# First group norm about an early average, constants on ScalarE's queue, half chunks, and first patches loaded behind their own block's store

## What is computed

```python
def _gn(v, G=32, eps=1e-5):           # group norm: 32 groups of 12 channels
    g = v.reshape(B_, G, C_ // G, H_, W_)
    m = jnp.mean(g, axis=(2, 3, 4), keepdims=True)
    s = jnp.var(g, axis=(2, 3, 4), keepdims=True)
    return ((g - m) / jnp.sqrt(s + eps)).reshape(v.shape)

# x: 1 x 384 x 192 x 192 float32
x = x + _L0_conv_ref(_gn(x), ...)   # 1x1 conv to q, k, v; 2x2 max pool; 3x3 depthwise; channel attention
                                    # with four top-k softmaxes; gelu; doubling; 1x1 projection
x = x + _L1_conv_ref(_gn(x), ...)   # depthwise 13x13 + 3x3 + identity, each with a batch norm
```

## Time and profile before

| | us |
|---|---|
| median of three runs | 2852.78 |
| the profiled execution | 2850.55 |
| its span, first to last instruction | 2848.7 |
| TensorE busy (90%) | 2575.4 |
| VectorE busy (89%) | 2523.7 |
| ScalarE busy (52%) | 1483.0 |
| GpSimd busy (3%) | 84.8 |

### The profile page before, as it was taken

The page is one execution under the profiler, slowest core; times in us unless marked ns, Lnnn a source line. Parts: engine busy times, 40 slices in busy tenths (PEclk is TensorE's granted clock), DMA queues, the critical chain, the costliest instruction groups (busy, mean ns, idle before and its releaser), DMA issues. The chain is left out here.

```text
span 2848.7 us, 50909 instructions
## 1 busy us (share of the span) xinstructions
PE 2575.4 (90%) x17291; PEld 1861.9 (65%) x17291; DVE 2523.7 (89%) x3511; ACT 1483.0 (52%) x1920; POOL 84.8 (3%) x155
## 2 busy tenths in 40 slices
PE   0039999999999999999999599998599999999998
PEld 0026666666666666666666366666499999999997
DVE  7968999999999999999999799999688888888884
ACT  0043354555554644555423277777566666666663
POOL 0020000000000000000000100000200000000000
PEclk9999999999999999999999799999799999999999
DMA  8965112332323223313000499997999999999996
GB/s 332 416 212 175 62 34 85 102 97 70 91 86 109 74 86 103 97 69 91 34 17 7 171 357 357 362 361 281 249 278 291 288 289 290 296 295 294 290 287 184
DMA packets 346041, 546.38 MB, mean 192 GB/s; under 512 B 133536, under 2 KB 244896, under 8 KB 345888
## 3 DMA queue, kind: packets, MB, share of 16 engines
q1 hardware_dynamic: 321984, 465.80, 52.0%
q10 hardware_dynamic: 23424, 77.08, 8.0%
q0 software_dynamic: 480, 1.51, 0.2%
HBM read 363.88 MB, written 180.44 MB: 191 GB/s over the span
## 5 line engine op out<-in xcount | busy, mean ns | idle before, releaser
L774 PE MATMUL qk_qb<-qk_xhi,whi 128*128 128x384 f16 x2592 | 846.2, 326 | 19.6 <-DVE qk_xlo L670 14.3
L774 PE MATMUL qk_qb<-qk_xlo,whi 128*128 128x384 f16 x2592 | 846.2, 326 | 0.0
L774 PE MATMUL qk_qb<-qk_xhi,wlo 128*128 128x384 f16 x2592 | 846.2, 326 | 0.0
L691 DVE SCALAR_TENSOR_TENSOR qk_dw<-qk_pool,qk_wd,qk_dw 128x768 f32<-128x768 f32 (+2 forms) x864 | 837.8, 1010 | 2.0 <-ACT qk_dw L543 2.0
L678 DVE TENSOR_REDUCE qk_pool<-qk_qb 128x192 f32<-128x768 f32 x432 | 412.2, 954 | 65.8 <-PE qk_qb L774 49.2
L1674 PE MATMUL cv_cb<-cv_hi,cv_toep 128*128 128x288 f16 x1536 | 346.8, 286 | 30.0 <-DVE cv_lo_last L1606 22.9
L774 PEld LDWEIGHTS qk_qb<-qk_xhi,whi 128*128 128x128 f16 x2592 | 254.0, 98 | 182.8 <-DVE qk_xlo L670 16.1
L774 PEld LDWEIGHTS qk_qb<-qk_xhi,wlo 128*128 128x128 f16 x2592 | 253.9, 98 | 168.2 <-issue 1.0
L774 PEld LDWEIGHTS qk_qb<-qk_xlo,whi 128*128 128x128 f16 x2592 | 254.0, 98 | 162.8 <-issue 1.0
L1680 PE MATMUL cv_cb<-cv_hi_next,cv_toep 128*128 128x288 f16 x1536 | 346.0, 287 | 0.0
L1549 ACT ACTIVATE cv_res<-cv_cb,cv_cst 128x288 f32<-128x288 f32 x384 | 187.5, 502 | 298.7 <-PE cv_cb L1680 237.1
(11 more groups left out here) (182 smaller groups left out, 3532.4 us busy)
## 6 DMA issues: line engine op xcount, KB each, us to landing
cv_toep<-toeplitz_scratch SPq DMA_DIRECT2D x384, 256.0 KB, 6.6
cv_raw<-patch_scratch SPq DMA_DIRECT2D x192, 325.0 KB, 7.5
st_x<-in_x SPq DMA_DIRECT2D x24, 2304.0 KB, 17.1
qk_xf<-in_x SPq DMA_DIRECT2D x72, 768.0 KB, 4.2
pr_xb<-in_x SPq DMA_DIRECT2D x24, 2304.0 KB, 10.1
out<-cv_rows ACTq DMA_DIRECT2D x72, 768.0 KB, 7.1
patch_scratch<-pr_turned SPq DMA_DIRECT2D x39, 832.0 KB, 9.3
patch_scratch<-cv_raw SPq DMA_DIRECT2D x36, 832.0 KB, 9.2
```

Source lines behind the costliest of these rows:

```text
L691: V.scalar_tensor_tensor(acc, pool[:, o, r + y:r + y + n, x:x + PW], wd[:, o, k:k + 1], acc, ALU.mult, ALU.add).then_inc(taps_done, 1)
L774: ins = nc.tensor.matmul(qbank[s % NQB][:, h, 0:2 * W], w[:, b, o * P:(o + 1) * P], x[:, par, j // 2, b, at_row:at_row + 2 * W], start=n = ...
```

## The change

1. In the statistics, the 24 transfers of weights and constants are issued by ScalarE's queue at its start; SyncE's queue holds chunks alone.
2. VectorE's `wlo` and tap preparation stand behind chunk 11 instead of chunk 3.
3. `group_affine` is gone. Ahead of the last round VectorE sums the records' means of chunks 0 to 19, TensorE averages the sums over the groups while the last four chunks run; the deviations of all records are taken about this early average `base`, and one pass of averages over two columns (`cols`) gives the correction `off` and the variance. It stands at the head of `stage_qkv`. Averages skip the pairs of blocks that share no group (seven matmuls instead of nine), in the second norm too.
4. The first two chunks are split in halves, with norms shared between ScalarE (6) and VectorE (6). Chunk 1 has a place of its own in `dw` (`second`), loaded at the stage's start; so chunk 2's load waits for chunk 0 only. GpSimd clears `dw` and what follows only when all halves are split; ScalarE waits for `padw` at unit 1.
5. TensorE runs 24 matmuls behind the averages in the q/k/v stage and 48 transposes at the start of the depthwise stage whose results nobody reads.
6. `conv.first_load` stands behind the store of block 0, ahead of those of blocks 1 and 2.

```diff
@@ stage_statistics, sync @@
-            sp.dma_start(wst[:, :, :], wT.rearrange("(b p) n -> p b n", p=P)).then_inc(w_in, 16)
-            sp.dma_start(kern[:, :, :, :], w_large.rearrange("(b p) o y x -> p b (o y) x", p=P)).then_inc(c_in, 16)
...
-            ahead.constants(sp)
@@ stage_statistics, scalar @@
+            act.dma_start(wst[:, :, :], wT.rearrange("(b p) n -> p b n", p=P)).then_inc(w_in, 16)
...
+            ahead.constants(act)
             act.wait_ge(w_in, 16)
@@ stage_statistics, vector @@
             statistics(0)
+            with dve.Fori(1, ROUNDS // 2) as r:
+                statistics(r)
             dve.wait_ge(whi_ready, 1)
...
-            with dve.Fori(1, STEPS // XBUFS) as r:
+            with dve.Fori(ROUNDS // 2, ROUNDS - 1) as r:
                 statistics(r)
+            records = stats[:, :, :, :].rearrange("p b n (two s) -> p b (n two) s", two=2)
+            dve.wait_ge(x_used, (ROUNDS - 1) * XBUFS)
+            V.tensor_reduce(sums[:, :], records[:, :, 0:KNOWN, 1], AX.X, ALU.add).then_inc(sums_ready, 1)
+            statistics(ROUNDS - 1)
+            dve.wait_ge(guess_done, 1)
+            chained(V.tensor_scalar(base[:, :], guess[:, 0:CB], 1.0 / KNOWN, None, ALU.mult))
+            dve.wait_ge(x_used, STEPS)
+            chained(V.tensor_tensor(dev[:, 0], records[:, :, :, 1],
+                                    base[:, :].unsqueeze(2).broadcast_to([P, CB, 2 * STEPS * REC]), ALU.subtract))
+            chained(V.tensor_tensor(dev[:, 1], dev[:, 0], dev[:, 0], ALU.mult))
+            V.tensor_reduce(part[:, 0], records[:, :, :, 2], AX.X, ALU.add)
+            V.tensor_reduce(cols[:, :, 0], dev[:, 0], AX.X, ALU.add)
+            chained(V.tensor_reduce(part[:, 1], dev[:, 1], AX.X, ALU.add))
+            V.scalar_tensor_tensor(cols[:, :, 1], part[:, 0], 2.0 / 512, part[:, 1], ALU.mult, ALU.add)
@@ stage_qkv @@
+        PIECES = [(h, k) for h in range(HALF) for k in range(2)]
+        BY_DVE = ((0, 1), (1, 1), (1, 2), (2, 1), (3, 1), (3, 2))
@@ stage_qkv, sync @@
             for b in range(CB):
-                load(1, b)
+                start.load_into(sp, second[:, b], 1, b, x2_in[b])
             for b in range(CB):
-                load(2, b)
+                sp.wait_ge(lo_half, b + 1)
+                sp.wait_ge(lo_ready, b + 1)
+                start.load(sp, 2, b)
@@ stage_qkv, scalar @@
+            nc.scalar.activation(root[:, :], var[:, :], ACT.Sqrt, bias=eps[:, :], scale=UNSCALE).then_inc(root_ready, 1)
...
-            for h in range(HALF):
+            for n in range(2 * HALF):
                 for b in range(CB):
-                    norm(h, b)
-                    high(h, 0, h, b)
+                    if (n, b) in BY_ACT:
+                        early_norm(n, b)
+                for b in range(CB):
+                    early_high(n, b)
@@ stage_qkv, gpsimd @@
+            gp.wait_ge(lo_half, HALF * CB)
+            gp.wait_ge(lo_ready, HALF * CB)
             G.memset(dw[:, :, 0:PW], 0.0).then_inc(zeroed, 1)
@@ stage_qkv, vector: off, var and mean from averages, sx from root, then @@
-            for h in range(HALF):
+            early_norm(0, 1)
+            early_norm(1, 1)
+            early_norm(1, 2)
+            for b in range(CB):
+                early_low(0, b)
+            early_norm(2, 1)
+            for b in range(CB):
+                early_low(1, b)
+            early_norm(3, 1)
+            early_norm(3, 2)
+            for n in range(2, 2 * HALF):
                 for b in range(CB):
-                    low(h, 0, h, b)
+                    early_low(n, b)
@@ stage_qkv, tensor @@
+            for o in range(CB):
+                near = [b for b in range(CB) if abs(b - o) <= 1]
+                for b in near:
+                    ins = nc.tensor.matmul(averages[:, 2 * o:2 * o + 2], member[:, b, o * P:(o + 1) * P], cols[:, b, :],
+                                           start=b == near[0], stop=b == near[-1])
+            ins.then_inc(avg_done, 1)
+            for n in range(WARM):
+                nc.tensor.matmul(qbank[1][:, 0, 0:2 * W], whi[:, 0, 0:P], whi[:, 0, 0:2 * W],
+                                 start=n == 0, stop=n == WARM - 1)
@@ stage_project, sync @@
-            sp.wait_ge(stored[0][0], 16 * (STEPS // 2 + 1))
-            sp.wait_ge(stored[1][0], 16 * (STEPS // 2))
-            conv.first_load(sp)
+                if b == 0:
+                    sp.wait_ge(stored[0][0], 16 * (STEPS // 2 + 1))
+                    sp.wait_ge(stored[1][0], 16 * (STEPS // 2))
+                    conv.first_load(sp)
@@ stage_depthwise, tensor @@
+            WARM = 48
+            for n in range(WARM):
+                nc.tensor.transpose(bbank[0][:, n % TPB * P:(n % TPB + 1) * P], ident[:, :], ident[:, :])
```

More of the change, by code:

```diff
@@ L162, in stage_statistics @@
-def stage_statistics(nc, x3, stats, wT, whi, wlo, w_large, w_small, norms, kern, scale, shift, ident, place, member, ahead):
+def stage_statistics(nc, x3, stats, base, cols, wT, whi, wlo, w_large, w_small, norms, kern, scale, shift, ident, place, member, ahead):
     XBUFS = 4
     REC = CHUNK // 512
+    ROUNDS = STEPS // XBUFS
+    KNOWN = (ROUNDS - 1) * XBUFS * REC * 2
     with ExitStack() as ctx:
@@ L320, in qkv_start, with stage_qkv @@
     start.xf, start.bq, start.bd, start.wd, start.c_in, start.x_in = xf, bq, bd, wd, c_in, x_in
-    start.constants, start.load, start.first_load = constants, load, first_load
+    start.constants, start.load, start.load_into, start.first_load = constants, load, load_into, first_load
     return start
-def stage_qkv(nc, start, whi, wlo, mean, rstd, ident, kern, inv_norm, v_dram, toep_dram, edge_dram, gram):
+def stage_qkv(nc, start, whi, wlo, base, cols, member, ident, kern, inv_norm, v_dram, toep_dram, edge_dram, gram):
     HALF = 2
@@ L351, in stage_qkv @@
     BANKS = 2 * QK
+    RECORDS = STEPS * (CHUNK // 512) * 2
+    HALVES = CHUNK // 2
     with ExitStack() as ctx:
@@ L377, in stage_qkv @@
         tbank = [ps(f"tb{i}", [P, 512]) for i in range(NTB)]
+        off, sq, var, root, mean = sb("off", [P, CB]), sb("sq", [P, CB]), sb("var", [P, CB]), sb("root", [P, CB]), sb("mean", [P, CB])
+        eps = sb("eps", [P, 1])
+        averages = tbank[0]
+        second = dw[:, :, :].rearrange("p r n -> p (r n)")[:, 0:CB * CHUNK].rearrange("p (b n) -> p b n", b=CB)
+        x2_in = [sem(f"x2_in{b}") for b in range(CB)]
+        link, eps_ready, avg_done, var_ready, root_ready = (sem("link"), sem("eps_ready"), sem("avg_done"), sem("var_ready"),
+                                                            sem("root_ready"))
+        act_norm, dve_norm, hi_half, lo_half = sem("act_norm"), sem("dve_norm"), sem("hi_half"), sem("lo_half")
         prep, zeroed = sem("prep"), sem("zeroed")
@@ L417, in wait_taps, with early, early_loaded, early_normed @@
             eng.wait_ge(taps_done, tap_index(u, o, k) + 1)
+        PIECES = [(h, k) for h in range(HALF) for k in range(2)]
+        BY_DVE = ((0, 1), (1, 1), (1, 2), (2, 1), (3, 1), (3, 2))
+        BY_ACT = tuple((n, b) for n in range(2 * HALF) for b in range(CB) if (n, b) not in BY_DVE)
+        def early(n, b):
+            h, k = PIECES[n]
+            return (xf[:, b] if h == 0 else second[:, b])[:, k * HALVES:(k + 1) * HALVES]
+        def early_loaded(eng, n, b):
+            h, k = PIECES[n]
+            eng.wait_ge(x_in[b] if h == 0 else x2_in[b], 16)
+        def early_normed(eng, n, b):
+            if (n, b) in BY_DVE:
+                eng.wait_ge(dve_norm, BY_DVE.index((n, b)) + 1)
+            else:
+                eng.wait_ge(act_norm, BY_ACT.index((n, b)) + 1)
         def run(eng, step):
@@ L728, in _ @@
             GRAM_AT = {3: (0, 3), 5: (3, NPX + 1)}
+            WARM = 24
+            for o in range(CB):
+                near = [b for b in range(CB) if abs(b - o) <= 1]
+                for b in near:
+                    ins = nc.tensor.matmul(averages[:, 2 * o:2 * o + 2], member[:, b, o * P:(o + 1) * P], cols[:, b, :],
+                                           start=b == near[0], stop=b == near[-1])
+            ins.then_inc(avg_done, 1)
+            for n in range(WARM):
+                nc.tensor.matmul(qbank[1][:, 0, 0:2 * W], whi[:, 0, 0:P], whi[:, 0, 0:2 * W],
+                                 start=n == 0, stop=n == WARM - 1)
             def transposes(u, par, o):
@@ L1283, in averages @@
                 for o in range(CB):
-                    for b in range(CB):
+                    near = [b for b in range(CB) if abs(b - o) <= 1]
+                    for b in near:
                         ins = nc.tensor.matmul(bank[:, o:o + 1], member[:, b, o * P:(o + 1) * P], values(b),
-                                               start=b == 0, stop=b == CB - 1)
+                                               start=b == near[0], stop=b == near[-1])
                 ins.then_inc(done, 1)
```

131 lines of the change are left out of this document (66 added, 65 removed).

## The result

The changed kernel takes **2856.66 us** (median of 20 runs, 2852.73 to 2859.47) where the kernel before takes 2852.60 in as many (2849.92 to 2854.93). The ratio is 1.0015 with an interval of 1.0009 to 1.0022: no gain, 4.1 us later, where 18 us less were forecast. The profiled execution (2858.81, span 2857.1) is 8.3 us behind that of before; each lies some 2 us to its own side of its median, so the pair of traces shows twice the difference of the medians.

What follows compares the result with a forecast made beforehand. TensorE was taken to bound the q/k/v and steady depthwise stretches, so gains had to come ahead of them: 11.3 us up to and through q/k/v plus 7.0 at the patch loads, 18.3 in sum, median 2834.5 us, range 2825 to 2843.

Steps and rivals of the forecast that it cites:

- the first part of its sum: Everything from the statistics through the q/k/v stage: 11.3 us gained, between 8 and 14.5.
- Rival (e): Statistics: small packets take turns with the chunks' big ones, making statistics 30 us longer instead of 4; 2860 us, chance 0.05.
- Statistics without that wait: Statistics with constants on ScalarE's queue and preparation moved: end at 159.1 us instead of 162.6, 3.5 gained (0 to 7.5).
- Early average: Group norm, from last statistics to first norm: 8.2 us against 18.6, 10.4 gained.
- Halves: First chunks of q/k/v: slot 2 starts 16.5 us behind the first norm instead of 21.3, 4.9 gained.
- Blank stores, chunk 3: Early q/k/v: later blank stores delay chunk 3, so the 4.9 us gain becomes a 6.3 us TensorE stall.
- the clock: TensorE behind the stall at chunk 3's copy: half-speed matmuls lose 2.4 us (0 to 3).
- Patch loads: Start of the depthwise stage, loads behind the first store: VectorE starts 8.7 us earlier, 7.0 net (3 to 11).
- the term for GpSimd: Depthwise start: GpSimd's memset, copies and sends fall on VectorE's first pieces and the tap loads; 1.7 us taken off.

Runs made afterwards that it cites:

- e1: Changed kernel with the nine last small transfers issued by ScalarE behind `whi` and `std` instead of ahead of them: 2842.94 us, ratio 0.9970.
- e4: Changed kernel with the 24 transfers of weights and constants back in SyncE's queue, VectorE's preparation left behind chunk 11: 2840.55 us, ratio 0.9963.
- e5: e1 with VectorE's preparation moved from behind chunk 11 to behind chunk 15: 2833.16 us, ratio 0.9939.
- e9: e7 with VectorE's reductions of the first two slots put ahead of the last half chunk's lows: 2825.66 us, ratio 0.9909.
- e8: e5 with GpSimd held in the depthwise stage until VectorE's third low part is made: 2833.38 us.
- e2: Changed kernel with every statistics chunk loaded by two transfers of 3 KB rows instead of one of 6 KB rows: 2837.82 us, ratio 0.9952.
- e3: Kernel before with only the eight first patch loads moved behind the store of block 0: 2846.04 us, ratio 0.9981.
- e6: Changed kernel with the 24 transfers back in SyncE's queue and VectorE's preparation back behind chunk 3: 2838.84 us, ratio 0.9958.
- e7: e5 with SyncE issuing the blank stores behind chunk 3's loads instead of ahead of its first step: 2828.64 us, ratio 0.9925.
- e11: e7 with GpSimd held in the depthwise stage until VectorE's first low part is made: 2828.01 us.
- e10: e7 without the loop of 24 warm-up matmuls ahead of the first slot: 2830.21 us, ratio 0.9920.
- e12: e9 and e11 together, reductions ahead of the last lows and GpSimd held until the first low part: 2827.50 us, ratio 0.9910.

## Why the prediction was wrong

**The step that failed** is the last sentence of the first part of its sum: "ScalarE itself issues 24 more transfers, with nothing else queued until `whi`, needed at 86'". It counted who waits behind the issues and gave the issues no duration. Ready at 107.0 + 3.1 instead of before 86, `whi` cost 25.2 us of VectorE's wait (84.9 to 110.1). Of the miss of 22.2 us in the medians (2856.66 against 2834.5) that is all, and more; e1 and e4 gave part of it back, e5 21.5 to 23.5 us.

It could have been worked out. A norm's transfer is 384 rows, and a chunk is 384 rows of 6 KB: by turns, each norm lasts a chunk, 5.70 us. The weights, two kernel arrays and twelve norms are fifteen such lengths, 86 us, to the landing of the last norm (measured: 97.4), and the biases and `w_dw` with 1152 rows each are nine more, all of them issued ahead of `whi`. That ScalarE would stand at the issues themselves could be read from SyncE's rows above, 4.3 to 5.4 us each in the kernel before. Rival (e) had the taking of turns but asked only what it does to the big transfers. Its price there, 30 us, is refuted: chunks run at 5.86 against 5.70, the small packets' whole cost to them about 0.16 us a chunk. The small ones paid, and through them an engine. That the measured 2856.66 lies 3 us from this rival's 2860 is luck: it got there by another way.

**Statistics without that wait**: 183.03 - 25.20 = 157.8 as an estimate, forecast 159.1; e5, whose preparation waits for nothing, ended them at 159.3. Chunk 11 ended at 84.9, forecast 86.0. Right to 1.3.

**Early average**: 8.30 us from the last statistics to the first norm, forecast 8.2, in place of 18.6. Right.

**Halves**: slot 2 at +17.05 behind the first norm, forecast +16.5. Right, and so is the reason: VectorE's order sets it, as e9 showed by changing the order.

**Blank stores, chunk 3**: stores at +23.55 (+22.9), copy at +75.8 (+76.5), ScalarE's idle 16.9 (over 20). TensorE reached the copy at +72.8, not +70.2, so that its stall is 3.0 us and not 6.3. What held it up is a start of slot 2 that was 0.5 later than forecast, and the half speed behind the 5.16 us of idle ahead of it, from 208.38 to about 212.1, which costs 1.9: mis-sized, since the forecast put the clock only behind the later stall. From first norm to last q/k/v matmul the stage took 1376.95 us against 1376.47: 0.5 lost where 2.6 were reckoned.

**Patch loads**: alone 5.1 us in the runs, forecast 7.0 (3 to 11). VectorE's start was right (8.5 against 8.7); the term for GpSimd was too small. VectorE's first pieces, from first norm to first matmul, take 13.3 us instead of 10.0: 3.3 where 1.7 were taken off. In e8 they took 9.0 when GpSimd was held.

In the changed kernel VectorE starts 23.66 us behind the first store, as forecast (23 to 25). But from the last q/k/v matmul to that store it is 431.7 us in its profile and 427.6 in that of before. The same stretch takes 428.0 to 428.6 in the profiles of e2, e3, e4, e6, e7 and e11, and 431.4 to 431.7 in those of e1, e5, e8, e9, e10 and e12. Kernels that hold the changed q/k/v stage show both lengths; the two that do not, the kernel before and e3, show the short one, in one profile each. What decides between them, and whether the change makes the long one more frequent, stays open. It may be why the profiles are 8.3 us apart and the medians 4.1.

## What to carry to other kernels

A DMA issue is free only while its queue has room. Before small transfers are moved to another engine's queue, count their rows against the rows of the big transfers beside them: by turns, n small rows last as long as n big ones. Then ask what stands behind the issues in that engine's program, and behind the landings. Issue what is wanted first, do the work that is due, and put the rest after it; a consumer moved a little later (here by four chunks) costs nothing and takes the landing off the path.

And where an engine is started earlier, look at what the next waits are before paying for it: e8, e11 and the warm-up each did what they were meant to do locally, and no gain at the end shows in the runs. A collision that is only moved is paid for at its new place.

## What the runs showed of the hardware

- Two busy queues on the same 16 engines had equal numbers of rows served (1356 and 1356 in 20 us), although one had rows of 6 KB and the other of four bytes. A transfer of 384 four-byte rows took 5.6 us beside 6 KB rows, 3.0 beside 3 KB rows, and landed 31.1 and 18.8 us after its issue, against 2.2 with the engines idle.
- The small rows cost the big transfers 16 GB/s at 6 KB rows (418 alone, 402 beside them) and 26 at 3 KB (399 and 373).
- An engine's program stood at an issue when some five or six such transfers were in flight: ScalarE's for 5.6 us in the changed kernel, SyncE's for 4.3 to 5.4 us behind the first four chunks of the kernel before. With the engines idle an issue took 0.5 us. Whether the limit counts transfers or rows, no run tells.
- VectorE's copies of 1248 columns took 1.05 us beside GpSimd's work and 0.51 without it. Its first four norms took 5.28 us in e5 and 3.36 in e8, still beside GpSimd's memset of 1.80 us: one of the four took 2.10. With GpSimd idle four took 1.89. The Trainium skill (SBUF — State Buffer, "Who interferes with whom") describes that lock; these rows agree.
- TensorE's granted clock was at half for 3 to 5 us of its work behind idle times of 5.16 and 5.15 us (e7, e11) and of 3.02 (the changed kernel), and behind one of 2.66 that followed a slot at half speed (e10), but not behind one of 1.90 (e9). The same code gave 4.8 us in e7 and 3.2 in e11.
